# The scalings of a layer norm moved from the Vector engine to the Scalar engine, in an eight-layer transformer kernel

## What is computed

```python
def _layernorm(x, axis=-1, eps=1e-05):
    m = jnp.mean(x, axis=axis, keepdims=True)
    v = jnp.var(x, axis=axis, keepdims=True)
    return (x - m) / jnp.sqrt(v + eps)

x = x + tanh(g_xattn[0]) * L0_xattn(_layernorm(x), ctx)   # 16 heads of 8
x = x + tanh(g_ffn[0])   * L0_ffn(_layernorm(x))          # 8 experts, exact gelu, top 2
x = x + tanh(g_xattn[1]) * L1_xattn(_layernorm(x), ctx)   # 16 heads of 64
x = x + tanh(g_ffn[1])   * L1_ffn(_layernorm(x))          # 8 linear experts, softmax weights
x = x + tanh(g_xattn[2]) * L2_xattn(_layernorm(x), ctx)   # one head of 128
x = x + tanh(g_ffn[2])   * L2_ffn(_layernorm(x))          # 8 experts, silu, top 1
x = x + tanh(g_xattn[3]) * L3_xattn(_layernorm(x), ctx)   # 16 heads of 8
x = x + tanh(g_ffn[3])   * L3_ffn(_layernorm(x))          # ternary weights, gelu, inner norm
```

## Time and profile before

| | |
|---|---|
| median of 3 runs | 1339.56 us (1338.64 to 1340.12) |
| the profiled execution: time, span | 1334.05 us, 1331.9 us |
| PE busy, PEld busy | 87%, 69% of the span |
| DVE, ACT, POOL busy | 54%, 39%, 21% |
| mean granted clock of PE | 0.901 |

### The profile page before, as it was taken

The page is one execution under the profiler, slowest core; times in us unless marked ns, Lnnn a source line. Parts: engine busy times, 40 slices in busy tenths (PEclk is TensorE's granted clock), DMA queues, the critical chain, the costliest instruction groups (busy, mean ns, idle before and its releaser), DMA issues.

```text
span 1331.9 us, 18247 instructions
## 1 busy us (share of the span) xinstructions
PE 1153.2 (87%) x7149; PEld 915.4 (69%) x7149; DVE 718.6 (54%) x2149; ACT 523.5 (39%) x1012; POOL 275.9 (21%) x203
## 2 busy tenths in 40 slices
PE   3888989999999799999965598999999888988655
PEld 2766886767777687887843375777777666877555
DVE  7787774232232566666578842231313387778643
ACT  1544553343433264554500112343434244554354
POOL 6443442010100321221200200000000043544100
PEclk9889988999999899999977655999999978988787
DMA  7000000000000000000040000000000000000000
GB/s 208 1 1 1 1 1 13 13 17 0 1 1 1 28 1 1 1 1 1 1 126 0 1 1 0 0 1 1 1 0 1 17 1 1 1 0 1 0 16 16
DMA packets 22367, 16.10 MB, mean 12 GB/s; under 512 B 3466, under 2 KB 19657, under 8 KB 22281
## 3 DMA queue, kind: packets, MB, share of 16 engines
q1 hardware_dynamic: 22281, 14.93, 3.9%
HBM read 13.88 MB, written 1.05 MB: 11 GB/s over the span
## 4 chain that ended last, share of the span: by engine, by line
PE 74%; DVE 17%; ACT 4%; issue 3%; POOL 1%; DMA 0%; POOLq 0%; DVEq 0%; SPq 0%; ACTq 0%
PE banks L851 17%; PE banks L840 17%; PE banks L789 9%; PE banks L725 7%; DVE xn L1148 4%; PE banks L685 3%; PE banks L933 3%; PE banks L686 2%; PE banks L687 2%; PE banks L942 2%; DVE x L1510 2%; PE banks L952 2%; DVE q L1240 1%; ACT sh L509 1%; PE banks L694 1%
## 5 line engine op out<-in xcount | busy, mean ns | idle before, releaser
L576 ACT ACTIVATE hT<-banks,b 128x512 f32<-128x512 f32 x256 | 175.5, 687 | 272.5 <-PE banks L840 265.8
L851 PEld LDWEIGHTS banks<-wx,hT 128*128 128x128 f32 x2048 | 237.3, 192 | 23.0 <-issue 23.0
L1381 DVE SCALAR_TENSOR_TENSOR x<-banks,cw,x 128x128 f32<-128x128 f32 x256 | 72.1, 345 | 328.6 <-PE banks L851 328.6
L851 PE MATMUL banks<-wx,hT 128*128 128x128 f32 x2048 | 239.2, 275 | 0.0
L840 PE MATMUL banks<-xT,wx 128*128 128x512 f32 x512 | 235.4, 604 | 0.0
L404 POOL TENSOR_TENSOR sh<-sh,rd 128x616 f32<-128x616 f32 x96 | 116.7, 1216 | 283.9 <-DVE rd L1195 283.9
L840 PEld LDWEIGHTS banks<-xT,wx 128*128 128x128 f32 x512 | 94.3, 194 | 101.7 <-issue 101.4
L380 POOL TENSOR_TENSOR rstd<-vv,const 128x4 f32<-128x4 f32 x32 | 32.2, 1008 | 581.5 <-DVE vv L1140 581.5
L509 ACT ACTIVATE sh<-sh 128x308 f32<-128x308 f32 x192 | 81.2, 460 | 130.8 <-DVE sh L1185 130.8
L789 PE MATMUL banks<-prob,v 128*128 128x128 f32 x1024 | 120.6, 276 | 0.0
L725 PE MATMUL banks<-const,sh 128*77 128x128 f32 x768 | 115.1, 300 | 4.1 <-POOL sh L404 4.1
(11 more groups left out here) (297 smaller groups left out, 1614.5 us busy)
## 6 DMA issues: line engine op xcount, KB each, us to landing
wx<-in_L_ffn_W SPq DMA_DIRECT2D x16, 512.0 KB, 7.0
out<-x SPq DMA_DIRECT2D x4, 256.0 KB, 2.2
x<-in_x SPq DMA_DIRECT2D x1, 768.0 KB, 4.7
raw<-in_L_xattn_Wq SPq DMA_DIRECT2D x1, 512.0 KB, 3.5
raw<-in_L_ffn_expert_w SPq DMA_DIRECT2D x1, 512.0 KB, 5.4
wo<-in_L_xattn_Wo SPq DMA_DIRECT2D x1, 512.0 KB
ctok<-in_ctx SPq DMA_DIRECT2D x1, 462.0 KB
raw<-in_L_xattn_Wk SPq DMA_DIRECT2D x1, 384.0 KB, 3.4
```

Source lines behind the costliest of these rows:

```text
L576: act.activation(hT[j % 2][:, c, :], ps[:, c, :], func, bias=b1[2 * run][:, u:u + 1])\
L851: ins = pe.matmul(ps[:, 4 + j % 2, t * P:t * P + P], hT[j % 2][:, c, t * P:t * P + P], w_[:, 4 + e // 2, (4 * (e % 2) + c) * P:(4 * (e % 2 ...
```

## The change

x minus mean, times root, is the same as x times root plus a shift, with shift = -mean times root. DVE now computes only the shift of the four tiles, in one 128x4 instruction. ACT writes the four tiles of `xn` with four activations, `Identity` with a scale and a bias from SBUF, at the head of its own `front`. The semaphore `fr.xn`, for which PE waits, is raised by ACT; a new one, `fr.shift`, orders ACT behind DVE. The places of the calls in each engine's program are as before.

```diff
+        shift = place("shift", [P, GB])
...
-        fr = sems("front", "link", "var", "rstd", "xn", "xt", "hi", "lo")
+        fr = sems("front", "shift", "link", "var", "rstd", "xn", "xt", "hi", "lo")
...
             def front(n):
+                act.wait_ge(fr.shift, n + 1)
+                g_ = n % NG
+                for t in range(GB):
+                    ins = act.activation(xn[:, t, :], x[:, g_ * GB + t, :], ACT.Identity, scale=rstd[:, t:t + 1],
+                                         bias=shift[:, t:t + 1])
+                ins.then_inc(fr.xn, 1)
                 act.wait_ge(fr.xt, n + 1)
...
             def front_b(gn, n):
 
                 dve.wait_ge(fr.rstd, n + 1)
-                for t in range(GB):
-                    ins = dve.tensor_scalar(xn[:, t, :], x[:, bass.ds(gn * GB + t, 1), :].rearrange("p o d -> p (o d)"),
-                                            mv[:, t, 0:1], rstd[:, t:t + 1], ALU.subtract, ALU.mult)
-                ins.then_inc(fr.xn, 1)
+                dve.scalar_tensor_tensor(out=shift[:, :], in0=mv[:, :, 0], scalar=-1.0, in1=rstd[:, :], op0=ALU.mult,
+                                         op1=ALU.mult).then_inc(fr.shift, 1)
```

## The result

The changed kernel takes 1390.4 us (median; 1389.3 to 1391.4), the kernel before 1339.8 in the same session: a ratio of 1.0378, 95% interval 1.0360 to 1.0396, +50.6 us. The profiled execution after has a span of 1389.2 us.

The account below looks back on a forecast made before the run. PE mostly bounds the kernel, in program order, so later xn behind ACT's work is paid in full. Stage stalls plus clock losses sum to +52.1 us: 1339.6 + 52 = 1392 us, own range 1382 to 1402, with rivals 1375 to 1412.

Parts of the forecast that it names:

- Four activations: Every front: ACT's four scalings of xn take 1.6 us, between bounds of 1.50 and 1.8.
- that rival: Fronts outside the gelu stages: Identity brings two table loads each, 64 us more, 1456 us; chance 0.03.
- Start: First front: DVE no longer waits behind POOL's memset, first weight casts start at 17.10 instead of 20.21: -3.1 us.
- heads8: Eight fronts: xn behind ACT's last q copy, +0.55 each for seven, +2.2 at the second pass's first; +6.0 us.
- The 2 us for the clock: In heads8, where PE's clock already falls after each change of group: 2 us added for lower clock.
- experts: Eight fronts: PE waits 2.46 us for xn behind expert 4's hidden activations, never regained; +19.7 us.
- 5.1 of clock: In the experts: PE's clock falls after three of eight longer waits, +5.1 us; bounds none and 13.6.
- heads64: Four fronts: +0.5 us at the first, -0.56 each from the second on as waits for k1 copies go; -1.1 us.
- mixed: Four fronts: shift plus ACT's scalings take longer than DVE's, +0.7 us each; +2.8 us.
- head128 and ternary: PE waits for xn: 2.26 us behind head128's exponential, four times, +9.0; 3.86 behind ternary's affine activations, three times, +11.6.
- Relief wins: Rival: freeing DVE from POOL gains at most 35 us in heads8 and the start, 1305 us; chance 0.03.

Follow-up runs that it names:

- run 10: Kernel before with only the scalings of the very first front on ACT: 1335.1 us, ratio 0.9971.
- Run 8: Kernel before, all scalings on DVE, but in heads8 issued ahead of the key combinations, before POOL's products with the mask: 1321.6 us, ratio 0.9879.
- run 1: Changed kernel, but in the experts ACT issues the next group's scalings at expert 2, not behind expert 4's hidden activations: 1364.8 us, ratio 1.0191.
- run 2: Kernel before with only the eight fronts of the experts moved to ACT, at the place of the change: 1362.2 us, ratio 1.0167.
- run 11: Kernel before with only the four fronts of mixed on ACT: 1339.6 us, ratio 1.0005.
- run 5: Changed kernel with scalings moved ahead of the exponential in head128 and ahead of the first affine activations in ternary: 1370.9 us, ratio 1.0233.
- run 6: Changed kernel, all scalings on ACT, but issued early in heads8, experts, heads64, head128 and ternary: 1324.0 us, ratio 0.9884.
- run 3: Changed kernel with the scalings of the experts' eight fronts done twice, first into a tile nobody reads: 1407.7 us, ratio 1.0513.

## Why the prediction was right, term by term

The forecast was 1392, the time is 1390.4, and the mechanism is the one named: `xn` behind other ACT work, with PE's ordered program behind `xn`. That the total is met to 1.6 us is in part luck: several terms below are off by 1 to 2 us, in both directions. (The terms as written add up to 52.0, not to 52.1.)

- *Four activations.* Forecast 1.6 us, measured 1.63 to 1.67. The estimate from the Trainium skill, "ScalarE: Activation LUTs" (What ACT_TABLE_LOAD costs), 1.64, agrees with the trace; the row of the PSUM source that I leaned on (1.50) was a little low. No table load was added: the profile after has six again, so that rival is out.
- *Start.* -3.1; run 10 has -3.9, from -1.1 to -6.7. In the trace the first context product starts at 21.11 instead of 24.34. DVE's first cast, issued at 16.57, ended only at 17.34, so it was still held by the memset, as reckoned.
- *heads8.* 0.55 a front forecast, 0.58 seen; 2.2 at the first of the second pass, 1122.92 - 1118.26 = 4.66 against 1.99, so 2.7 seen. With the clock 8 forecast; 8.7 by taking it out, 4.4 by putting it in alone (2.8 to 5.9). The 2 us for the clock were not measured by themselves. Run 8 shows what the alternative is worth: the change gave DVE the relief and took it back behind ACT's copies.
- *experts.* A wait of 2.46 forecast, 2.40 seen at each of eight. 19.7 + 5.1 of clock = 24.8; 25.0 by run 1, 22.4 by run 2. The groups grew by 61.33 - 58.74 = 2.59, 0.19 more than the wait, which no row here explains; the clock fell behind two fronts, not three, at 1.6 each, not 1.7. The two misses cancel.
- *heads64.* -1.1 forecast: +0.5 for the first group and -0.56 for each of the others. In the traces the distances from one front to the next, from the last of the experts on, changed by +0.2, +0.6, -0.6 and -0.6, together -0.4. What the sum left out is the clock here: at the first front PE waits 1.79 us for `xn`, the clock behind it is 0.72 over 6 us, and the first eight products of the scores (L940) take 2.42 us, where before they took 1.30 at clock 1.00. The stage had no run of its own.
- *mixed.* +2.8 forecast, +0.7 (-0.7 to +2.1) by run 11: the term that was too large. The later `xn` is in the trace (in its first group ACT's scalings start at 693.61 and PE's transposes at 695.31, 1.70 us, where it was 679.37 - 678.21 = 1.16 with DVE's, and the shift comes ahead), so the delay is there, 0.7 us a front as forecast. By the traces the stage loses even more and keeps it to the end (run 11), by the medians it doesn't. Why the two differ stays open.
- *head128 and ternary.* 9.0 + 11.6 = 20.6 forecast, 19.4 by run 5. Waits of 2.22 and 3.67 us against 2.26 and 3.86.
- *Do the parts add?* Taken out of the changed kernel, experts, heads8 and head128 with ternary are 25.0 + 8.7 + 19.4 = 53.1; with -3.9, -0.4 and +0.7 for the rest this is 49.5 of the 50.6. Put in alone, experts and heads8 give 7 us less. The intervals of the four ratios and of the changed kernel's together leave more than 8 us to either side, so all of the 7 may be error.

"Relief wins" was the rival on the other side. It failed at the place that it named: it needed less than 1.1 us for a front on the average, and the 15 fronts of the experts, `head128` and `ternary` made PE wait 2.2 to 3.7. It isn't absurd, though: once the places are repaired (run 6), ACT does all the scalings and the kernel is faster.

## What to carry to other kernels

Before work is moved to an engine that is mostly idle, ask what stands ahead of it in that engine's program at that point, and who stands behind its result; a share of busy time answers neither. Issue the moved work as soon as its inputs are there, ahead of the copies or activations that wait for the bound engine: here the place alone is worth 66 us, from 4% slower to 1% faster. And before moving it at all, see if a few lines further up on its own engine it escapes what it waits for: that gave 16 of the 20 us.

Don't book differences of a few us between two single traces to a stage: compare a stretch that is the same code first, and see how far the traces already differ there.

## What the runs showed of the hardware that was not expected

- What POOL holds up on DVE goes by the form of the instruction. The scalings (tensor_scalar, both tensors in SBUF) lasted until POOL's products had ended; the `q` combinations (scalar_tensor_tensor, one of the two tensors in PSUM) ran in 0.75 us each inside them (run 8), the same as behind them, and POOL's two products took 4.54 us beside the one and 4.51 beside the other. The Trainium skill, "SBUF — State Buffer" (Who interferes with whom), says this: tensor_scalar can enter a mode that takes the ports shared with GpSimd, and an instruction outside such modes with at most one input in SBUF doesn't contend. The traces agree on both counts, and the rule would have pointed to run 8 as the cheaper repair from the start. No run here separates the operation from the place of its input. The copies from PSUM at the start, 1.63 us for four inside a memset, are a second case: they have a single source like the casts from SBUF, the first of which lasted 0.77 us instead of 0.35, to the memset's end.
- Equal programs come to full clock at unequal times in the start-up phase, with a difference of 2.7 us at the next front, and the clock column doesn't show it: it stands at 1.00 while the products take 0.63 us instead of 0.40 (run 10).
- Waits of PE of 2.40 us in an otherwise full stretch brought the clock down behind two of eight, waits of 3.94 behind eight of eight, at 1.6 us for each fall (run 3). Which two of the eight it is differs from kernel to kernel (runs 2 and 3).
